# Where the last sum of a quantised feed-forward stage is made, and who lowers its reciprocals

## The reference

```python
def fp4_quant_dequant(x):
    xb = x.reshape(shape[:-1] + (shape[-1] // 16, 16))
    scale = jnp.maximum(jnp.max(jnp.abs(xb), axis=-1, keepdims=True) / 6.0, 1e-12)
    xn = xb / scale
    q = _GRID[jnp.searchsorted(_MID, jnp.abs(xn))] * jnp.sign(xn) * scale
    return q.reshape(shape)
gate, up = fp4_linear(x, w_gate), fp4_linear(x, w_up)      # 256 -> 704
y = fp4_linear(jax.nn.silu(gate) * up, w_down)             # 704 -> 256
...
x = x + attention(layernorm(x), ctx_1024)
x = x + ffn(layernorm(x))
```

## Time and profile before

| | |
|---|---|
| median of 3 runs | 473.12 us (472.83 to 474.83) |
| profiled execution, its own time | 472.21 us |
| its span, first to last instruction | 470.0 us |
| mean granted TensorE clock | 0.967 |
| PE busy | 395.4 us (84%) |
| DVE busy | 385.3 us (82%) |
| ACT busy | 273.9 us (58%) |
| POOL busy | 208.5 us (44%) |
| stores to `out` | 16 of 128 KB, issued by SP |

### The profile page before, as it was taken

One profiled execution on the slowest core, in us unless ns is written; L12 is line 12 of the kernel. 1 busy time (PEld: TensorE's weight loads), 2 busy tenths in 40 slices (PEclk: granted clock), 3 DMA queues, 4 the chain that ended last, 5 costly groups with the idle time before them and its releaser, 6 DMA issues.

```text
span 470.0 us, 10216 instructions
## 1 busy us (share of the span) xinstructions
PE 395.4 (84%) x3581; PEld 308.4 (66%) x3581; DVE 385.3 (82%) x766; ACT 273.9 (58%) x855; POOL 208.5 (44%) x177
## 2 busy tenths in 40 slices
PE   1889759979979989989889799998767887887965
PEld 1658538867758768768678588886435665665754
DVE  2799887896996997977978969877859889898792
ACT  3597647747756766667487478767243464444431
POOL 7240133254253352532533443422455777878751
PEclk9999988999999999989999999999778999999998
DMA  7950000000000000000000000000000000000011
GB/s 243 316 190 1 2 0 1 2 1 3 1 0 0 0 0 0 0 0 0 0 0 0 1 1 0 2 1 0 1 1 0 13 23 11 11 22 11 24 33 35
DMA packets 8406, 11.18 MB, mean 24 GB/s; under 512 B 499, under 2 KB 6335, under 8 KB 8383
## 3 DMA queue, kind: packets, MB, share of 16 engines
q1 hardware_dynamic: 8383, 10.88, 7.3%
HBM read 8.78 MB, written 2.10 MB: 23 GB/s over the span
## 4 chain that ended last, share of the span: by engine, by line
DVE 40%; PE 28%; issue 12%; POOL 9%; ACT 6%; DMA 1%; DVEq 1%; POOLq 1%; SPq 0%; ACTq 0%
PE ps L357 7%; PE ps L358 7%; PE ps L359 7%; DVE negmax L923 5%; PE ps L457 3%; DVE xn L873 3%; DVE arena L935 3%; DVE arena L914 3%; POOL arena L1192 3%; PE ps L449 3%; DVE vw L868 2%; POOL arena L1234 2%; DVE arena L979 2%; ACT arena L677 2%; POOL arena L1238 1%
## 5 line engine op out<-in xcount | busy, mean ns | idle before, releaser
L1184 POOL TENSOR_TENSOR arena<-arena,rinv 128x616 f32<-128x616 f32 x64 | 77.7, 1214 | 174.1 <-DVE rinv L931 174.1
L677 ACT ACTIVATE arena<-ps,ebias 128x154 f32<-128x154 f32 x256 | 96.2, 397 | 37.9 <-DVE ebias L926 37.5
L357 PE MATMUL ps<-vw,arena 128*128 128x256 f16 (+1 forms) x352 | 98.0, 278 | 23.9 <-DVE xs L943 10.7
L358 PE MATMUL ps<-vw,arena 128*128 128x256 f16 (+1 forms) x352 | 97.8, 278 | 0.0
L359 PE MATMUL ps<-vw,arena 128*128 128x256 f16 (+1 forms) x352 | 97.8, 278 | 0.0
L687 ACT ACTIVATE arena<-ps 128x512 f16<-128x512 f32 x80 | 48.4, 605 | 31.5 <-PE ps L457 30.9
L935 DVE TENSOR_TENSOR arena<-ps,arena 128x512 f16<-128x512 f32 x80 | 54.1, 676 | 8.6 <-ACT arena L687 8.0
L357 PEld LDWEIGHTS ps<-vw,arena 128*128 128x128 f16 x352 | 34.8, 99 | 33.7 <-DVE arena L935 20.3
L357 PE MATMUL ps<-arena,xnT_h 128*128 128x352 f16 x128 | 42.8, 335 | 15.3 <-DVE xnT_l L1022 13.3
L677 ACT ACTIVATION_READ_ACCUMULATOR arena<-ps,ebias 128x1 f32 x256 | 54.8, 214 | 0.0
L923 DVE TENSOR_REDUCE negmax<-ps 128x4 f32<-128x616 f32 x64 | 50.6, 790 | 2.8 <-PE ps L449 1.6
(11 more groups left out here) (136 smaller groups left out, 946.3 us busy)
## 6 DMA issues: line engine op xcount, KB each, us to landing
out_dram<-arena SPq DMA_DIRECT2D x16, 128.0 KB, 1.7
xs<-in_x_dram SPq DMA_DIRECT2D x2, 896.0 KB, 10.1
arena<-in_L_xattn_w_out_dram SPq DMA_DIRECT2D x1, 1024.0 KB, 6.4
wffn<-in_L_ffn_w_down_dram SPq DMA_DIRECT2D x1, 704.0 KB, 8.0
wffn<-in_L_ffn_w_gate_dram SPq DMA_DIRECT2D x1, 640.0 KB, 10.9
wffn<-in_L_ffn_w_up_dram SPq DMA_DIRECT2D x1, 640.0 KB, 5.6
vw<-in_ctx_dram SPq DMA_DIRECT2D x1, 308.0 KB
xs<-in_x_dram SPq DMA_DIRECT2D x2, 128.0 KB, 4.9
```

The source lines that it names most:

```text
L357: pe.matmul(o, a_h, b_h, start=start, stop=False)
L358: pe.matmul(o, a_h, b_l, start=False, stop=False)
L677: last = act.activation(prob[:, s, h * L:(h + 1) * L], ps[:, 2 * (j % 2) + k % 2, (k // 2) * L:(k // 2 + 1) * L], ACT.Exp, bias=ebias[:, s ...
L1184: pool.tensor_tensor(v, v, rinv[:, s, 4 * j:4 * j + 4].unsqueeze(2).to_broadcast([P, 4, L]), ALU.mult).then_inc(normed, 1)
```

## The change

- The clamp of the block scales of x and of the hidden values is a `scalar_tensor_tensor` that takes its lower bound from a tile `least`, in place of a `tensor_scalar` with a constant. The weights' scales keep `block_scales`.
- The lowering of the reciprocals, L1190 on GpSimd, becomes a fourth operation on VectorE, a `scalar_tensor_tensor` with a tile of zeros, behind the reciprocal (`lowered_scales`). GpSimd's `value` waits for that one and goes straight to its product.
- ScalarE's `y_copy` and GpSimd's `add_x1` become one `scalar_tensor_tensor` on VectorE that reads `D_BANK` and `xs` and writes `y`. It stands behind `h_low` in VectorE's order. `down` now waits for `y_ready`, which that operation signals.

```diff
-        below = sb("below", [P, 1], F32)
+        least = sb("least", [P, F // BLOCK], F32)
+        zeros = sb("zeros", [P, F // BLOCK], F32)
...
             def down(i, s):
                 t = 2 * i + s
                 pe.wait_ge(ht_low, t + 1)
-                wait(pe, y_copied, t)
+                wait(pe, y_ready, t)
...
-            def y_copy(i, s):
-
-                act.wait_ge(down_mm, 2 * i + s + 1)
-                wait(act, stored[s], 16 * i)
-                act.activation(y[:, s], ps[:, D_BANK, 0:D], ACT.Copy, scale=1.0 / (HS * FS)).then_inc(y_copied, 1)
...
-                    if exists(summed[0]): y_copy(*summed)
...
             h_high(*step_of(last - 2))
-            y_copy(*step_of(last - 3))
             act.wait_ge(down_mm, last - 2)
             h_high(*step_of(last - 1))
-            y_copy(*step_of(last - 2))
             act.wait_ge(down_mm, last - 1)
             h_high(*step_of(last))
-            y_copy(*step_of(last - 1))
-            y_copy(*step_of(last))
...
+            def lowered_scales(src, r, done, t):
+
+                amax, scale, inv, lowered = r
+                n = amax.shape[1]
+                dve.tensor_reduce(amax, blocks(src), AX.X, ALU.max, apply_absolute_value=True).then_inc(done, 1)
+                dve.wait_ge(done, 4 * t + 1)
+                dve.scalar_tensor_tensor(scale, amax, SIXTH, least[:, 0:n], ALU.mult, ALU.max).then_inc(done, 1)
+                dve.wait_ge(done, 4 * t + 2)
+                dve.reciprocal(inv, scale).then_inc(done, 1)
+                dve.wait_ge(done, 4 * t + 3)
+                dve.scalar_tensor_tensor(lowered, inv, BELOW, zeros[:, 0:n], ALU.mult, ALU.add).then_inc(done, 1)
...
-                block_scales(both(xnorm), [blk_x[:, r] for r in range(3)], xscaled, i)
+                lowered_scales(both(xnorm), [blk_x[:, r] for r in range(4)], xscaled, i)
...
+            def add_x1(i, s):
+                dve.wait_ge(down_mm, 2 * i + s + 1)
+                wait(dve, stored[s], 16 * i)
+                dve.scalar_tensor_tensor(y[:, s], ps[:, D_BANK, 0:D], 1.0 / (HS * FS),
+                                         xs[:, s, bass.ds(i, 1), :].rearrange("p o d -> p (o d)"),
+                                         ALU.mult, ALU.add).then_inc(y_ready, 1)
...
-                block_scales(hid[:, s], [blk_h[:, s, r] for r in range(3)], hscaled, t)
+                lowered_scales(hid[:, s], [blk_h[:, s, r] for r in range(4)], hscaled, t)
...
-                    if last_tile(i, s): h_low(*shift(i, s, -TURN_LAG))
+                    if last_tile(i, s):
+                        h_low(*shift(i, s, -TURN_LAG))
+                        add_x1(*shift(i, s, -DOWN_LAG))
                     if exists(shift(i, s, -1)[0]): grid_h(*shift(i, s, -1))
                     if last_tile(i, s):
                         h_low(*shift(i, s, -2))
-                    elif exists(shift(i, s, -TURN_LAG)[0]):
-                        h_low(*shift(i, s, -TURN_LAG))
-                    if last_tile(i, s): quantise_last(i, s)
+                        add_x1(*shift(i, s, -TURN_LAG))
+                        quantise_last(i, s)
+                    else:
+                        if exists(shift(i, s, -TURN_LAG)[0]): h_low(*shift(i, s, -TURN_LAG))
+                        if exists(shift(i, s, -DOWN_LAG)[0]): add_x1(*shift(i, s, -DOWN_LAG))
 
             steps(dve, ffn, first=2, last=STEPS - 2)
             for t in range(2 * STEPS - 2, 2 * STEPS):
                 h_low(*step_of(t))
+                add_x1(*step_of(t - 1))
+            add_x1(*step_of(2 * STEPS - 1))
...
-            def value(v, src, r, scaled, lowered, valued, t):
-
-                pool.wait_ge(scaled, 3 * t + 3)
-                pool.tensor_tensor(r[3], r[2], below[:, :].to_broadcast([P, r[2].shape[1]]), ALU.mult).then_inc(lowered, 1)
-                pool.wait_ge(lowered, t + 1)
-                pool.tensor_tensor(blocks(v), blocks(src), spread(r[3]), ALU.mult).then_inc(valued, 1)
+            def value(v, src, lowered, scaled, valued, t):
+                pool.wait_ge(scaled, 4 * t + 4)
+                pool.tensor_tensor(blocks(v), blocks(src), spread(lowered), ALU.mult).then_inc(valued, 1)
...
-            def add_x1(i, s):
-                pool.wait_ge(y_copied, 2 * i + s + 1)
-                pool.tensor_tensor(y[:, s], y[:, s], xs[:, s, bass.ds(i, 1), :].rearrange("p o d -> p (o d)"),
-                                   ALU.add).then_inc(y_ready, 1)
...
-                    if exists(shift(i, s, -DOWN_LAG)[0]): add_x1(*shift(i, s, -DOWN_LAG))
```

More of the change, by code:

```diff
@@ L224, in xattn_ffn_kernel @@
         wt_mm, wt_high, wt_low, pad2_zero = sem("wt_mm"), sem("wt_high"), sem("wt_low"), sem("pad2_zero")
-        xcentred, xnormed, xscaled, xvalued, xlowered = sem("xcentred"), sem("xnormed"), sem("xscaled"), sem("xvalued"), sem("xlowered")
+        xcentred, xnormed, xscaled, xvalued = sem("xcentred"), sem("xnormed"), sem("xscaled"), sem("xvalued")
         xmagic, xsummed, xgrid, xq_done = sem("xmagic"), sem("xsummed"), sem("xgrid"), sem("xq_done")
@@ L228, in xattn_ffn_kernel @@
         gu_mm, silu_done, hid_ready = sem("gu_mm"), sem("silu_done"), sem("hid_ready")
-        hscaled, hlowered, hvalued = sem("hscaled"), sem("hlowered"), sem("hvalued")
+        hscaled, hvalued = sem("hscaled"), sem("hvalued")
         hmagic, hsummed, hgrid, hq_done = sem("hmagic"), sem("hsummed"), sem("hgrid"), sem("hq_done")
@@ L233, in xattn_ffn_kernel @@
         ht_mm, ht_high, ht_low = sem("ht_mm"), sem("ht_high"), sem("ht_low")
-        down_mm, y_copied, y_ready = sem("down_mm"), sem("y_copied"), sem("y_ready")
+        down_mm, y_ready = sem("down_mm"), sem("y_ready")
         stored = [sem("stored0"), sem("stored1")]
@@ L1123, in quantise_last @@
                 dve.wait_ge(hq_done, t - 1)
-                dve.wait_ge(hscaled, 3 * t + 3)
+                dve.wait_ge(hscaled, 4 * t + 4)
                 then(dve.tensor_tensor(blocks(v), blocks(hid[:, s]), spread(blk_h[:, s, 2]), ALU.mult), 1)
@@ L1158, in _ @@
                 h_low(*step_of(t))
+                add_x1(*step_of(t - 1))
+            add_x1(*step_of(2 * STEPS - 1))
         @block.gpsimd
         def _(pool):
-            pool.memset(below[:, :], BELOW)
+            pool.memset(least[:, :], 1e-12)
+            pool.memset(zeros[:, :], 0.0)
             pool.memset(ident[:, :], 0.0).then_inc(ident_zero, 1)
@@ L1185, in norm @@
                                    ALU.mult).then_inc(normed, 1)
-            def value(v, src, r, scaled, lowered, valued, t):
-                pool.wait_ge(scaled, 3 * t + 3)
-                pool.tensor_tensor(r[3], r[2], below[:, :].to_broadcast([P, r[2].shape[1]]), ALU.mult).then_inc(lowered, 1)
-                pool.wait_ge(lowered, t + 1)
-                pool.tensor_tensor(blocks(v), blocks(src), spread(r[3]), ALU.mult).then_inc(valued, 1)
+            def value(v, src, lowered, scaled, valued, t):
+                pool.wait_ge(scaled, 4 * t + 4)
+                pool.tensor_tensor(blocks(v), blocks(src), spread(lowered), ALU.mult).then_inc(valued, 1)
             def value_x(i):
-                value(x_tmp[0], both(xnorm), [blk_x[:, r] for r in range(4)], xscaled, xlowered, xvalued, i)
+                value(x_tmp[0], both(xnorm), blk_x[:, 3], xscaled, xvalued, i)
             def round_x(i):
@@ L1227, in value_h @@
                 t = 2 * i + s
-                value(h_tmp[s][0], hid[:, s], [blk_h[:, s, r] for r in range(4)], hscaled, hlowered, hvalued, t)
+                value(h_tmp[s][0], hid[:, s], blk_h[:, s, 3], hscaled, hvalued, t)
             def round_h(i, s):
@@ L1246, in ffn @@
                     if exists(shift(i, s, -1)[0]): round_h(*shift(i, s, -1))
-                    if exists(shift(i, s, -DOWN_LAG)[0]): add_x1(*shift(i, s, -DOWN_LAG))
             steps(pool, ffn, first=2, last=STEPS - 2)
-            for t in range(2 * STEPS - DOWN_LAG, 2 * STEPS):
-                add_x1(*step_of(t))
 _INS = ['x', 'ctx_1024', 'L0_xattn_proj_q', 'L0_xattn_bias_q', 'L0_xattn_proj_k', 'L0_xattn_bias_k',
```

## The result

The changed kernel takes 478.07 us (median of 18 runs, 474.61 to 480.16), the kernel before 472.23 (18 runs beside it). The ratio is 1.012, 95% interval 1.0099 to 1.014: about 5.8 us slower. Forecast was 476.2, +3.1. The profiled execution took 479.98 us for a span of 478.2. Some executions of a kernel run over 1.5% longer than its fastest one, at a lower granted clock; they are left out of every time in this document.

What follows compares the result with a forecast made beforehand. VectorE and its port shared with GpSimd were taken to bound the feed-forward stage; -0.2 to (3,0), +1.5 for three pairs, +0.9, +1.0, +0.65 and -0.72 gave about +3.1, so 476.2 us, range 470 to 480.

Steps and rivals of the forecast that it cites:

- What bounds and what excludes: Feed-forward stage: VectorE and TensorE busiest; a GpSimd product and a VectorE operation with two SBUF tensors wait for each other.
- Who gets the port: Between VectorE's two grid steps: waiting GpSimd goes first, so without L1190 L1192 enters and L1014 takes about 2.0, not 0.89.
- The walk: Timing of one steady feed-forward pair, operation by operation: first tile loses 0.9 us, second wins 0.4, pair 16.82 for 16.32.
- Rival A: VectorE keeps the port between L1012 and L1014: pair 16.0, kernel 472 to 473.5; chance 0.15.
- The list of signs: What the profile would show: L1014 (h) about 2.0 us once in each tile, x clamp over 0.8, pair of 16.8.
- Added work: VectorE, per pair: two sums 0.66 us, three lowered reciprocals 0.9, clamps at the same price; about 1.6 against 1.36 idle.
- The first pairs: Feed-forward start to (3,0): first x chain 0.6 earlier, `h_low` of (0,0) 0.2 later, second half -0.4; -0.2 us at (3,0).
- rival D: New TensorE idle stretches of some 1.4 and 1.7 us bring the low clock: 484 to 488 us; chance 0.08.
- The bank: The down product waits for `y_ready`, 0.32 later: slack of about 0.9 us in steady pairs, +1.0 from (6,1) to (7,1).
- The last tile and the end: Last tile +0.65 us (later `h_low`, two sums, less waits); end -0.72, as L1238 goes and the sum replaces the copy.
- B: Small two-tensor VectorE operations don't wait for the port: 0.6 us won a pair, kernel 473.2, no change; chance 0.12.
- C: GpSimd sets the pace, its products coming before L1012: pair 14.3 us, kernel 463, half of it 468; chance 0.1.

Runs made afterwards that it cites:

- a filler: Changed kernel plus a GpSimd product of 44 or 32 zeros into scratch, ahead of first tiles' h product and the x product: 473.45 us, 1.0019 to the kernel before.
- the two kernels that shortened the first tile alone: Changed kernel with, in first tiles only, `h_low` and sum before the grid steps (478.14 us), or a 44-number scratch GpSimd product before the h product (479.56 us).
- the order in both tiles: Changed kernel with `h_low` and the sum moved ahead of VectorE's two grid steps in both tiles of a pair: 475.94 us, 1.0069 to the kernel before.
- the wide filler: Changed kernel plus scratch GpSimd products of 512 columns ahead of first tiles' h product and the x product: 480.94 us, 1.0165 to the kernel before.

## Why the prediction was right in its direction and short in its size

**What bounds and what excludes: right.** VectorE sets the pace of the steady pairs; a GpSimd product and a VectorE operation with two SBUF tensors exclude each other. The Trainium skill's rule (SBUF — State Buffer, section on the two separate sides) says that the one that starts first has the shared ports for the whole instruction; the traces agree, with 0.88 us for a clamp of 32 numbers behind a product.

**Who gets the port: right, and the step that carried the forecast.** The walk had the long product in the gap and the second grid step at 1.96 in first tiles and 1.66 in second ones; measured 1.96, in every first tile from (1,0) on, and 1.63. (The list of signs said about 2.0 for each tile, which the walk doesn't.) Rival A would have shown 0.89. Taking the gap away by a filler gave back 1.02 us in the first tile. The price of L1190 was thus negative: it cost GpSimd 0.8 us of waiting and saved VectorE a wait of 1.1.

**Added work: right in kind, a little short in size.** From the start of the reciprocal to that of the next VectorE operation it was 0.34 us before (397.12 to 397.46) and is 0.59 now (401.33 to 401.92): 0.25 for the lowering, where the walk had 0.22. The clamp's next start comes 0.02 later, and the first grid step takes 0.89 where the walk kept 0.83; why it is longer is open. First tile 6.87 for a forecast of 6.75, second 10.25 for 10.07, pair +0.80 for +0.50: over three pairs 0.9 us of the miss.

**The first pairs: the step that failed most.** Forecast -0.2 at (3,0), measured +0.5 (53.57 against 53.05 us behind the first `hidden`). The step is "the first x chain comes 0.6 earlier". The chain did gain, 0.80 us up to its first grid step (14.71 against 15.51 us behind the first `hidden`). But there, too, a product stood ready for the gap, GpSimd's rounding product L1247, and the forecast for the first pairs had not asked who takes the gap between the two x grid steps:

```profile
343.07 0.69 DVE L1014 SCALAR_TENSOR_TENSOR arena<-arena 128x512 f32<-128x512 f32 x1
343.79 1.76 DVE L1016 SCALAR_TENSOR_TENSOR arena<-arena 128x512 f32<-128x512 f32 x1
```

```profile
343.20 1.80 POOL L1247 TENSOR_TENSOR arena<-arena,blk_h 128x704 f32<-128x704 f32 x1 [0.83 <-DVE arena L1016]
```

In the kernel before, that product had come earlier, the first x step had waited for its end (1.20) and the second took 0.69; now it is 0.69 and 1.76. That takes 0.56 back, and (1,0) comes only 0.24 earlier. In (1,1), `h_low` of (0,0) starts 0.94 later behind `hidden` than before (7.46 against 6.52 us; the walk's figures give 0.82), so it comes 0.7 later in all, not 0.2 (0.82 less 0.6). So most of this miss is a step of the kind that the walk had for the h grid steps and the forecast left out for the first x ones. TensorE waits for that `h_low`:

```profile
362.80 0.27 PE L358 MATMUL ps<-arena 128*128 128x256 f16 x1 [3.30 <-DVE arena L1144]
```

3.30 us where it was 2.36. The `hidden` that this sets comes 8.85 us behind the start of that product in both kernels (362.80 to 371.65, before 359.23 to 368.08), so the low clock there cost before what it costs now, and rival D doesn't explain this part of the miss. From (2,1) to (3,0) 0.19 is then won, not 0.4.

**The bank.** Steady pairs had room for it, as forecast. In the tiles where TensorE sets the pace, (6,1) to (7,1), the loss is 1.23 us (14.28 against 13.05), forecast 1.0.

**The last tile and the end.** Forecast +0.65 and -0.72, measured +0.32 and -0.17. The last tile gained more, since its int32 step and the one behind it run without GpSimd's sums beside them, 0.53 us each where they had taken 0.93. Now, and then before with the sums, which overlap both:

```profile
463.64 0.53 DVE L1135 TENSOR_SCALAR arena<-arena 128x704 int32<-128x704 int32 x1
464.21 0.53 DVE L1136 TENSOR_SCALAR arena<-arena 128x704 f32<-128x704 f32 x1
```

```profile
454.06 0.93 DVE L1126 TENSOR_SCALAR arena<-arena 128x704 int32<-128x704 int32 x1
455.03 0.93 DVE L1127 TENSOR_SCALAR arena<-arena 128x704 f32<-128x704 f32 x1
...
453.24 2.34 POOL L1238 TENSOR_TENSOR arena<-arena,xs 128x256 f32<-128x256 f32 x2
```

That is 0.8 us which the forecast did not have. It hides that the rest of the tile went 0.5 worse than forecast (its first `h_low` came 1.2 later and not 0.9), so the small error here is partly luck.

At the end the step "L1238 goes, the new sum stands in for the copy" overlooked a queue: the sum of tile 13 stands ahead on VectorE, and TensorE's down product of tile 14 waits for it.

```profile
468.98 0.37 PE L358 MATMUL ps<-arena 128*128 128x256 f16 x1 [0.54 <-DVE arena L1109]
```

The product starts 1.47 us behind the end of L1140, before 1.34: 0.13. Another 0.5 is the product itself, 3.7 us in place of 3.2, with more of it at the clock's lower level (matmuls of 0.42 us for 0.27).

**The sum.** End of attention 0.23, first pairs 0.52, three pairs 2.41, (6,0) to (6,1) 1.03, to (7,1) 1.23, last tile 0.32, end -0.17: 5.57 us in the profiles, 5.8 in the medians. The forecast of 3.1 lacked 0.95 in the first pairs and the end of attention, 0.9 in the steady pairs, 0.13 and 0.23 in the two stretches behind them and 0.55 at the end, less 0.33 in the last tile.

**The other rivals.** B (small operations don't wait): the x clamp took 0.88 in five of six pairs; in the first it took 0.23, starting 0.17 before the product ended. C (GpSimd sets the pace): its L1205 asks 0.15 behind the start of the first grid step (402.07 and 401.92). D (the clock): not in the changed kernel's steady pairs, which are granted 1.00 with idle stretches of 1.85 and 2.07 (and over 380 to 384 us, with one of 2.37 just ahead of them); but it makes the 0.5 in the down product of tile 14. At 3.08 it came every time, in the two kernels that shortened the first tile alone.

## What to carry to other kernels

A small GpSimd operation can be worth more than its time: where GpSimd and VectorE compete for the port, look at who asks during a VectorE instruction, because it runs next, for its full length, whatever stands behind on VectorE. Before removing one, find which instruction will ask in its place and how long it is. Judge the two halves of such a change by themselves: here the sum on VectorE alone is 0.6% faster than the kernel before, and the lowering beside it turned that into 1.2% slower. And walk TensorE's idle time along: a gain on VectorE that gathers it in one stretch can be lost to the clock.

## What was not expected of the hardware

- A filler that computes nothing of use made the kernel 4 to 5 us faster than the one without it (1.0019 against 1.012).
- TensorE idle for 1.85 and 2.07 us in each pair kept the 2.4 GHz level (granted 1.00). Idle for 3.08 us it fell to 0.50 behind all eight such stretches of two kernels. Between these it went either way: with the order in both tiles 1.00 stayed behind three stretches of 2.38 and fell to 0.50 behind another (over 414 to 416 us); with the wide filler it fell behind two of four of 2.44 or 2.45. Twelve useless transposes, 1.47 us of work, brought back 1.00 and took 1.3 us off a pair of 17.75.
- Two `tensor_scalar` operations on 704 columns of the last tile took 0.53 us where they had taken 0.93, with GpSimd's sums beside them gone.
